# Half-empty filter blocks of two groups share one matmul, with tiles copied within SBUF; statistics by batch at the start of the convolutions; normalised rows gathered

## The reference

```python
def reference(x, ...):                       # x: (4, 512, 16, 32)
    x = x + _L0_conv_ref(_gn(x), gate_w, w1, w2, w3)
    x = x + _L1_conv_ref(_gn(x), w3, w7, w15, w_mix)
    x = x + _L2_conv_ref(_gn(x), ...)        # the same form, other weights
    x = x + _L3_conv_ref(_gn(x), ...)
    return x
```

## Time and profile before

| | |
|---|---|
| median of 3 runs | 1094.27 us (1093.65 to 1095.57) |
| the profiled execution | 1094.17 us, of which 1092.2 from the first to the last instruction |
| PE busy | 1040.1 us |
| DVE, ACT, POOL busy | 501.0, 318.4, 126.3 us |
| mean granted TensorE clock | 0.976 |
| experts, up to the last down product | about 705 us |
| convolutions | about 705 to 1092 us |

### The profile page before, as it was taken

One profiled execution on the slowest core, in us unless ns is written; L12 is line 12 of the kernel. 1 busy time (PEld: TensorE's weight loads), 2 busy tenths in 40 slices (PEclk: granted clock), 3 DMA queues, 4 the chain that ended last, 5 costly groups with the idle time before them and its releaser, 6 DMA issues.

```text
span 1092.2 us, 14489 instructions
## 1 busy us (share of the span) xinstructions
PE 1040.1 (95%) x5315; PEld 870.7 (80%) x5316; DVE 501.0 (46%) x700; ACT 318.4 (29%) x435; POOL 126.3 (12%) x169
## 2 busy tenths in 40 slices
PE   5589999999999999999999999779999999999998
PEld 3278888888888888888888888668888988898887
DVE  4794154155136155245164372266236942587011
ACT  2412144144144244144144352114201320122122
POOL 2031111111111211111111122100000000000000
PEclk9859999999999999999999999979999999999999
DMA  8309216943972985953976949755373466436474
GB/s 346 126 20 340 48 29 241 390 158 145 389 253 68 399 320 213 393 183 116 410 269 259 392 149 400 241 216 186 128 231 132 148 231 224 148 117 246 153 222 116
DMA packets 69792, 240.16 MB, mean 220 GB/s; under 512 B 6272, under 2 KB 36096, under 8 KB 55360
## 3 DMA queue, kind: packets, MB, share of 16 engines
q1 hardware_dynamic: 61536, 216.62, 52.1%
q0 software_dynamic: 8080, 23.07, 9.0%
q10 hardware_dynamic: 144, 0.02, 0.0%
HBM read 136.15 MB, written 107.74 MB: 223 GB/s over the span
## 4 chain that ended last, share of the span: by engine, by line
PE 83%; DVE 7%; issue 4%; DMA 3%; SPq 1%; ACT 1%; POOLq 0%; DVEq 0%; ACTq 0%; POOL 0%
PE gate_ps L977 15%; PE up_ps L977 15%; PE y_ps L964 10%; PE head_ps L1466 9%; PE head_ps L1470 9%; PE head_ps L1467 9%; PE y_ps L967 5%; PE hT_ps L989 2%; PE xT_ps L954 1%; PE xT_ps L886 1%; SPq L409 1%; DMA block_row<-in_x,fetch 1%; DVE scaled L1267 1%; DVE split L1277 1%; PE turn_ps L1416 1%
## 5 line engine op out<-in xcount | busy, mean ns | idle before, releaser
L1466 PE MATMUL head_ps<-split,ring 128*128 128x256 f32 (+1 forms) x657 | 225.4, 343 | 1.4 <-ACT split L1158 1.2
L1470 PE MATMUL head_ps<-split,ring 128*128 128x256 f32 (+1 forms) x657 | 220.6, 336 | 0.0
L1467 PE MATMUL head_ps<-split,ring 128*128 128x256 f32 (+1 forms) x657 | 220.1, 335 | 0.0
L977 PE MATMUL gate_ps<-front 128*128 128x512 f32 x560 | 177.3, 398 | 1.8 <-DVE xT_lo L810 1.7
L977 PE MATMUL up_ps<-front 128*128 128x512 f32 x560 | 173.8, 392 | 0.0
L1466 PEld LDWEIGHTS head_ps<-split,ring 128*128 128x128 f32 x657 | 124.4, 189 | 15.4 <-issue 2.1
L1470 PEld LDWEIGHTS head_ps<-split,ring 128*128 128x128 f32 x657 | 124.3, 189 | 14.6
L1467 PEld LDWEIGHTS head_ps<-split,ring 128*128 128x128 f32 x657 | 124.6, 190 | 13.6
L827 DVE TENSOR_TENSOR hidden<-silu,up_ps 128x1024 f32<-128x1024 f32 x35 | 42.8, 1222 | 177.9 <-ACT silu L586 177.9
L977 PEld LDWEIGHTS up_ps<-front 128*128 128x128 f32 x560 | 105.7, 189 | 22.9
L977 PEld LDWEIGHTS gate_ps<-front 128*128 128x128 f32 x560 | 102.9, 189 | 22.2 <-DVE xT_lo L810 2.1
(11 more groups left out here) (189 smaller groups left out, 1164.7 us busy)
## 6 DMA issues: line engine op xcount, KB each, us to landing
filters<-rows SPq DMA_DIRECT2D x56, 1568.0 KB
w_raw<-in_w13T SPq DMA_DIRECT2D x32, 1024.0 KB, 7.1
ring<-filters SPq DMA_DIRECT2D x15, 1920.0 KB, 7.9
w_raw<-in_w2T SPq DMA_DIRECT2D x16, 1024.0 KB, 5.2
ring<-filters SPq DMA_DIRECT2D x21, 768.0 KB, 4.7
ring<-filters SPq DMA_DIRECT2D x12, 1152.0 KB, 6.0
rows<-in_x SPq DMA_DIRECT2D x4, 1024.0 KB, 8.1
rowed<-acc SPq DMA_DIRECT2D x4, 1024.0 KB, 6.1
```

Of the source, the lines that this page charges most:

```text
L977: last = nc.tensor.matmul(o[:, n, :], a[:, k, :], b[:, k, t, n * 512:(n + 1) * 512], start=(k == 0 and a is xT_hi and b is w13_hi), stop=( ...
L1466: nc.tensor.matmul(place, kernel_hi, x_hi, start=(u == 0 and a == 0), stop=False)
L1467: nc.tensor.matmul(place, kernel_lo, x_hi, start=False, stop=False)
L1470: last = nc.tensor.matmul(place, kernel_hi, x_lo, start=False, stop=(u == len(units) - 1 and a == windows(s) - 1))
```

## The change

Three things.

**Shared half blocks.** Of a head's three units two have the same scale (`head_shared`). Their last windows, of which only partitions 64 to 127 count, become one product: partitions 64 to 127 hold the first one's filters and values, 0 to 63 the second one's. The filters are loaded into the two halves of a window of `ring` by two more DMAs of SP. The values are copied from partitions 64 to 127 of `split` into `shared` (4 slots) by POOL's DMAs, two for a task of 512 columns and four for one of 256, once the pieces are written and the slot is free. The three shared matmuls come last in a head and wait for them. A head thus has 5, 7, 8, 10 or 14 windows, and `ring` has 36 windows with new places.

**Statistics by batch at the beginning of the convolutions.** SP loads batch 0's rows when their own last block is added, then batch 1's. The filters of the second head wait for batch 1's rows. DVE does sums, centring and the subtraction batch by batch (`lane_sums`, `lane_centre`), then the factor for both (`lane_scale`). PE does a `lane_means` per batch and one `lane_deviations`, for batches 2 and 3 within the third task.

**Normalised rows gathered.** SP writes the normalised x to DRAM (`normal`) while routing runs, and POOL gathers blocks from there. `find_lanes`, `expand_lanes` and `normalise_rows` are gone. `find_weights` moves from the first block to its front, `take_targets` and `take_weights` ahead of the split of weight chunks 1 and 2, and that ahead of the low part of the first `xT`. POOL's copy of x to `acc` waits for x instead of the first expert's weights.

```diff
...
+def head_shared(h):
+    units = head_units(h)
+    return (0, 1) if units[0][0] == units[1][0] else (1, 2)
+def head_parts(h):
+    return [(s, j, windows(s) - (m in head_shared(h))) for m, (s, j) in enumerate(head_units(h))]
 def head_runs(h):
-    for s, j in head_units(h):
-        if runs and runs[-1][0] == s:
+    for s, j, n in head_parts(h):
+        if runs and runs[-1][0] == s and runs[-1][4] == n:
-            runs.append([s, j, 1, taken])
-        taken += windows(s)
+            runs.append([s, j, 1, taken, n])
+        taken += n
 def head_windows(h):
-    return sum(windows(s) for s, _ in head_units(h))
+    return sum(n for _, _, n in head_parts(h)) + 1
...
                if layer == l and same_batches(part, pair) and any(group == j for _, group in head_units(h)))
-RING = 48
-RING_PLACE = {11: 0, 12: 15, 6: 30, 13: 0, 14: 15, 15: 30, 10: 0, 7: 15, 8: 30, 9: 39, 0: 0, 1: 6, 2: 15, 3: 24, 4: 30, 5: 36}
+RING = 36
+RING_PLACE = {11: 0, 12: 14, 6: 28, 13: 0, 14: 14, 15: 0, 10: 14, 7: 28, 8: 0, 9: 16, 0: 8, 1: 24, 2: 0, 3: 14, 4: 19, 5: 28}
 for _i, (_l, _h) in enumerate(HEAD_SEQUENCE):
...
             if RING_PLACE[_head] < _at + head_windows(_h) and _at < RING_PLACE[_head] + head_windows(_head)]
-    RING_COUNT.append((_l + 1) * len(head_runs(_h)))
+    RING_COUNT.append((_l + 1) * (len(head_runs(_h)) + 2))
+SHARED = 4
+SHARED_AT = {h: i % SHARED for i, h in enumerate(HEAD_ORDER)}
+SHARED_PARTS = {None: (slice(0, 2),), 0: (slice(0, 1), slice(1, 2)), 1: (slice(0, 1), slice(1, 2))}
+SHARED_AFTER, SHARED_COUNT = [], []
+for _n, (_l, _h, _pair) in enumerate(TASKS):
+    SHARED_AFTER.append(max((_m + 1 for _m, (_, _head, _part) in enumerate(TASKS[:_n])
+                             if SHARED_AT[_head] == SHARED_AT[_h] and same_batches(_part, _pair)), default=None))
+    SHARED_COUNT.append(2 * len(SHARED_PARTS[_pair]) * sum(SHARED_AT[_head] == SHARED_AT[_h] and _part == _pair for _, _head, _part in TASKS[:_n + 1]))
...
             for k in range(KD):
+            for b in range(BATCH):
+                sp.wait_ge(normed, b + 1)
+                sp.dma_start(normal_rows[b], rows[:, b * QUARTERS:(b + 1) * QUARTERS, 0:D]).then_inc(normal_out, 16)
             for half in range(2):
+            sp.wait_ge(normal_out, 16 * BATCH)
...
-            pool.wait_ge(w13_in[KD - 1], 16)
+            pool.wait_ge(x_in[BATCH - 1], 16)
...
-                if isinstance(g, int):
-                    take_weights()
-            def new_expert(e, g0):
-                split_w13(e, g0, range(KD // 2))
-                normalise_rows(g0 + 1)
-                split_w13(e, g0, range(KD // 2, KD))
-            expand_lanes(0)
+            expand_weights()
-            expand_lanes(1)
-            take_lanes()
-            normalise_rows(0)
-            split_w13(0, 0, [1])
+            take_targets()
+            take_weights()
+            split_w13(0, 0, [1, 2])
-            split_w13(0, 0, range(2, KD))
-            expand_weights()
-            take_targets()
+            split_w13(0, 0, [3])
-            all_blocks(dve, new_expert, body, after_first)
+            all_blocks(dve, split_w13, body, after_first)
...
                 if RING_AFTER[i] is not None:
-                for s, j0, n, taken in head_runs(h):
-                    at, width = (RING_PLACE[h] + taken) * 2 * P, windows(s) * P
+                for s, j0, n, taken, count in head_runs(h):
+                    at, width = (RING_PLACE[h] + taken) * 2 * P, count * P
+                at = (RING_PLACE[h] + head_windows(h) - 1) * 2 * P
+                for half, m in zip((1, 0), head_shared(h)):
+                    s, j, count = head_parts(h)[m]
+                    begin = SCALE_AT[s] + count * P
+                    sp.dma_start(ring[half * P // 2:(half + 1) * P // 2, at:at + 2 * P].bitcast(f32).rearrange("p (a n) -> p a n", n=P),
+                                 filter_rows[P // 2:P, 2 * (l * GROUPS + j):2 * (l * GROUPS + j + 1), begin:begin + P]).then_inc(ring_in[h], 16)
-            wait_apart(sp, lasting.added, sp.value_load(table[0:1, E:E + 1], min_val=16, max_val=16 * (MAX_BLOCKS + 1)), lasting.sp_passed)
-            load_rows(0)
-            load_rows(1)
+            for b in range(PAIR):
+                wait_apart(sp, lasting.added, sp.value_load(table[0:1, E + b:E + b + 1], min_val=16, max_val=16 * (MAX_BLOCKS + 1)), lasting.sp_passed)
+                load_rows(b)
+            sp.wait_ge(rows_in[PAIR - 1], 16)
...
+        @block.gpsimd
+        def _(pool):
+            def share(n):
+                l, h, pair = TASKS[n]
+                slot, bs = SHARED_AT[h], batches(pair)
+                piece = l * len(PIECES) + max(PIECE_OF[head_units(h)[m][1], pair] for m in head_shared(h)) + 1
+                pool.wait_ge(high_ok, piece)
+                pool.wait_ge(low_ok, piece)
+                if SHARED_AFTER[n] is not None:
+                    pool.wait_ge(head_done, SHARED_AFTER[n])
+                for half, m in zip((1, 0), head_shared(h)):
+                    j = head_units(h)[m][1]
+                    for parts in SHARED_PARTS[pair]:
+                        pool.dma_start(shared[half * P // 2:(half + 1) * P // 2, slot, parts, bs.start:bs.stop, LEAD:LEAD + P].bitcast(f32),
+                                       split[P // 2:P, j, parts, bs.start:bs.stop, LEAD:LEAD + P].bitcast(f32)).then_inc(shared_in[slot, pair], 16)
+            for n in range(len(TASKS)):
+                share(n)
         def _(act):
...
                 for q in range(QUARTERS):
-            def lane_steps(pair):
-                at = LANE_STEPS * pair
-                dve.wait_ge(lane_step, at + PAIR * QUARTERS)
-                for b in range(PAIR):
-                    nc.vector.bn_aggr(lane[:, b, :], bn[:, b, :, :].rearrange("p q s -> p (q s)")).then_inc(lane_step, 1)
-                if pair == 0:
-                    nc.vector.memset(split[:, :, :, :, 0:LEAD].bitcast(f32), 0.0).then_inc(split_zeroed, 1)
-                group = lane_group[:, PAIR * pair:PAIR * (pair + 1), :]
-                dve.wait_ge(lane_stat, 2 * pair + 1)
-                nc.vector.tensor_copy(group.rearrange("p b s -> p (b s)"), stat_ps[:, 0, 0, 0:2 * PAIR]).then_inc(lane_step, 1)
-                dve.wait_ge(lane_step, at + PAIR * QUARTERS + PAIR + 1)
-                nc.vector.tensor_tensor(lane_dev[:, :], lane[:, :, 0], group[:, :, 0], ALU.subtract).then_inc(lane_step, 1)
-                dve.wait_ge(lane_step, at + PAIR * QUARTERS + PAIR + 2)
-                nc.vector.tensor_tensor(lane_dev2[:, :], lane_dev[:, :], lane_dev[:, :], ALU.mult).then_inc(lane_step, 1)
-                if pair == 0:
+                dve.wait_ge(lane_step, LANE_SUMMED[b] - 1)
+                nc.vector.bn_aggr(lane[:, b % PAIR, :], bn[:, b % PAIR, :, :].rearrange("p q s -> p (q s)")).then_inc(lane_step, 1)
+            def lane_centre(b):
+                n = b % PAIR
+                dve.wait_ge(lane_stat, LANE_MEANS[b])
+                nc.vector.tensor_copy(lane_group[:, b, :], stat_ps[:, 0, 0, 2 * n:2 * n + 2]).then_inc(lane_step, 1)
+                dve.wait_ge(lane_step, LANE_BEGUN[b] + 1)
+                nc.vector.tensor_tensor(lane_dev[:, n:n + 1], lane[:, n, 0:1], lane_group[:, b, 0:1], ALU.subtract).then_inc(lane_step, 1)
+                dve.wait_ge(lane_step, LANE_BEGUN[b] + 2)
+                nc.vector.tensor_tensor(lane_dev2[:, n:n + 1], lane_dev[:, n:n + 1], lane_dev[:, n:n + 1], ALU.mult).then_inc(lane_step, 1)
+                if b == 0:
-                for b in range(PAIR):
-                    at = (PAIR * pair + b) * P
-                    nc.vector.tensor_scalar(stream[:, :, at:at + P].rearrange("p j (q d) -> p j q d", d=HD),
-                                            rowed[:, PAIR * pair + b].rearrange("p q (j d) -> p j q d", d=HD),
-                                            group[:, b, 0:1], None, ALU.subtract).then_inc(first_ok, 1)
-                    if b == 0:
-                        dve.wait_ge(lane_stat, 2 * pair + 2)
-                        nc.vector.scalar_tensor_tensor(lane_var[:, :], stat_ps[:, 1, 0, 0:PAIR], EPS, group[:, :, 1], ALU.add, ALU.add).then_inc(lane_step, 1)
+                nc.vector.tensor_scalar(stream[:, :, b * P:(b + 1) * P].rearrange("p j (q d) -> p j q d", d=HD),
+                                        rowed[:, b].rearrange("p q (j d) -> p j q d", d=HD),
+                                        lane_group[:, b, 0:1], None, ALU.subtract).then_inc(first_ok, 1)
+            def lane_scale(pair):
+                dve.wait_ge(lane_stat, (PAIR + 1) * (pair + 1))
+                nc.vector.scalar_tensor_tensor(lane_var[:, :], stat_ps[:, 1, 0, 0:PAIR], EPS, lane_group[:, PAIR * pair:PAIR * (pair + 1), 1],
+                                               ALU.add, ALU.add).then_inc(lane_step, 1)
...
+            nc.vector.memset(split[:, :, :, :, 0:LEAD].bitcast(f32), 0.0).then_inc(split_zeroed, 1)
+            lane_centre(0)
-            lane_steps(0)
```

(39 more changed lines are left out.)

96 lines of the change are left out of this document (32 added, 64 removed).

## The result

| | before | after |
|---|---|---|
| median of four runs beside each other | 1094.92 us | 1126.64 us (1123.81 to 1137.7) |
| ratio, 95% interval | | 1.0306 [1.0254, 1.0359] |
| profiled execution, its span | 1094.17, 1092.2 | 1126.88, 1125.2 |

What follows compares the result with a forecast made beforehand. The convolutions were taken as bound by TensorE's number of matmuls and the columns they stream. The terms summed to -23.6 us from 1094.17, so 1070.6, stated as 1070; range 1057 to 1088.

Steps and rivals of the forecast that it cites:

- the ring's term: Filter loads through the ring cut from 48 to 36 windows, beside the copies: +1 us per layer, +3.0 in all.
- Rival B: Copies and ring loads meet, heads 12, 13 and 15 start late, 4 us per layer: 1079 us; chance 0.17.
- Full tasks: Copies for tasks of 512 columns: covered because pieces are written a task or more ahead; cost nothing.
- boundaries: Start of a new layer's half tasks, waiting for copies: +3.5 us at each of two boundaries, +7.0.
- first layer: First convolution layer's waits for copies: +2.4 us at head 12 and +1.9 at the second pair's first head.
- E+14.4: Head 11's forecast finish at a layer's start; E is the end of head 5, first pair, at 840.7 us.
- Matmuls removed: Three matmuls less per task in the convolutions, over three layers: -34.1 us where TensorE is the limit.
- Parts 2 and 3: Statistics by batch (-3.9 us at the convolutions' start, +1.5 for the second pair) and normalised rows gathered (-1.4).
- First head matmul: Start of the convolutions: about 717.3 us instead of 721.14, a gain of 3.9 us.
- the wait at the deviation matmul: Within head 6, TensorE stopped about 1.6 us for batch 2's whole subtraction; +1.5 us in the sum.
- The experts' start: First expert matmul at 76.4 us instead of 75.12, as VectorE splits weight chunks 1 and 2 first: +1.3.
- Rival A: POOL's queue becomes the bound at layer boundaries: +31 us each, about 1135; chance 0.08 for 1094 and above.

Runs made afterwards that it cites:

- spread: The changed kernel with every copy taken from and written to every other partition instead of the upper 64; 1081.0 us, ratio 0.9884.
- nocopy36: The changed kernel without copies, shared tiles filled once with zeros, ring still of 36 windows; 1068.3 us, ratio 0.9759 to the kernel before.
- ring40: The changed kernel with a ring of 40 windows and three shared slots instead of 36 and four; 1109.1 us, ratio 1.0135 to the kernel before.
- nocopy48: The changed kernel without copies, one zero-filled shared slot, and the ring of 48 windows in its old places; 1066.5 us, ratio 0.9736.
- best: The kernel pool with the last layer's outputs turned back later on TensorE; 1060.8 us, ratio 0.9693 to the kernel before.
- pool: The changed kernel with every copy into the shared tiles made by GpSimd itself instead of by DMA; 1074.5 us, ratio 0.9811.
- mixed: The changed kernel with the upper half of each shared tile copied by GpSimd itself, the lower half still by DMA; 1082.9 us, ratio 0.9890.
- stall: The kernel before, with head 15's filters in every layer loaded only when head 14 is done; 1124.0 us, ratio 1.0276.

## Why the prediction was wrong, step by step

**The step that failed is the ring's term,** "+1 us per layer, +3.0; bounds 0 and +4 per layer". It measured 34.4 us of waits, 11.5 a layer. Its reason had the bytes right, "8.4 MB per layer in runs of 512 bytes against 2.1 MB of windows saved", and went from them straight to "there is room on average". I never turned the bytes into DMA time, and the page of before had a price. Its q0 line, shown above, is 23.07 MB for 9.0% of 16 engines, 14.7 bytes per ns, where q1 gives 23.8. The copies' 25.2 MB at q0's price are 107 us of all engines in 371 us: 0.29 on top of 0.52. Measured were 0.84. That the two prices lie so close is partly luck: q0 of before holds gathers and accumulating writes of another kind, and the same copies cost 19.2 bytes per ns in spread. A share of 0.84 on average was 1.07 from 805 to 850 us, and a load with the 9.7 us of one head as its cover can't take 16.7.

**Rival B named the right place at a third of the size,** 4 us per layer against 11.5, and without the clock. It took one load of 10.3 us as the worst case, and called the ring the cause. The ring is innocent by itself (nocopy36), but it leaves less cover, so that delays become waits (ring40 takes back 17 us). What the copies cost beside a ring of 48 was not measured. "Full tasks: I cost these at nothing" is the same mistake seen from the other side. No full task's copy was late by itself, as I said; it made something else late.

**The second thing left out is the clock.** I priced waits by their idle time. PE is busy 351.6 us after and 332.3 in nocopy48 with the same 1933 instructions: 19.4 us of lower clock behind 46 us of waits. My list of signs did hold "a granted clock of 0.5 inside a layer", with no price beside it.

**The sum with what was measured:** ring +31.4 over its term, clock +19.4, boundaries +3.2 and first layer +0.8 (next point) make 54.8 of the 56.0 us. The matmuls' +3.3 and a start 1.2 earlier than forecast bring it to 56.9. That it closes within a microsecond is partly luck, since the boundaries' +3.2 is read off the first of the two alone.

**Boundaries.** Predicted +3.5 each. From the first matmul of head 3, second pair, to that of head 13 the kernel before takes 36.5 us (840.53 to 877.01), after 38.3 (851.91 to 890.24), and 3.2 less than before should be possible: +5.1. (At the second boundary it is 40.9 us, with a drop of the clock among them.) Head 11 ended at E+17.5, not E+14.4, since copies landed in 6.0 us beside the loads, not in 2 to 3. In nocopy48 the same stretch still takes 35.1 and in best 35.9: of the half tasks' 3.2 us, 1.8 and 2.6 are lost here even without DMA copies, and 1.7 of them are the wait of a total (`stat_ps`) for DVE's partial sums. The copies of the change cost the rest. The first layer's two waits were 2.4 and 2.7; I had 2.4 and 1.9.

**Matmuls removed.** Predicted -34.1, measured -30.8 in PE's busy time. A full head 13 takes 9.7 us from its first to its last matmul, as the prediction's sign asked. In best, which has no long wait, it is -31.9 (363.0 less 331.1); where the other 2.2 us went is open.

**Parts 2 and 3.** Predicted -3.8 in all, measured -3.4. First head matmul at 716.14 (717.3 predicted), the wait at the deviation matmul 1.5 (1.6). The 717.3 didn't follow from its own terms: they put the reciprocal 3.4 us earlier than before, which gives 717.8. The experts' start was missed: first expert matmul at 77.12, not 76.4, since the first rows came late, not DVE's splits. PE at that place after:

```profile
74.59 1.12 PE L928 MATMUL xT_ps<-ident,block_row 128*128 128x128 f32 x4 [4.57 <-DMA block_row<-normal,fetch]
77.12 1.22 PE L951 MATMUL gate_ps<-front 128*128 128x512 f32 x2 [1.41 <-DVE xT_lo L805]
```

**Rival A fell.** POOL's plain DMAs took 621 ns each (x204), beside a VectorE busy with two-input operations; 0.7 had been my figure. (Its +31 per boundary was also a slip: 59 less 26 is 33.) Of the two readings of the Trainium skill, "SBUF — State Buffer", Who interferes with whom, that the prediction set side by side, the trace agrees with the second: no starving beside `tensor_tensor`. But 1.09 us per DMA as the only way in which copies could hurt was too narrow.

**Left open.** Nocopy36 and nocopy48 stay 10 us and more above what I had worked out. Two waits and PE's busy time hold most of it in nocopy48, but why the turning back waits for ScalarE so much longer than before was followed only in pool. Copies issued from SP's or ACT's queue were not tried. Whether the average share or the partitions that copies and loads have in common makes the loads late was not separated.

## What to carry to other kernels

Price every new transfer in DMA-engine time, with the bytes per ns that the page's queue lines give for its kind, and add that share to the share of the stretch in which it runs. With the share near 1, loads with one step of cover become waits (11 in this kernel), and a wait of 7.4 us cost a third more through the clock. Here the copies within the on-chip store that touched half of the partitions were best left to an engine that had nothing to do.

## What the runs showed of the hardware that I had not expected

- A copy of 64 neighbouring partitions by DMA moved 13.9 bytes per ns of an engine, of 64 spread ones 19.2; the length of the runs made less of it (512 bytes 13.9, up to 4224 bytes 15.5).
- GpSimd copied 64 x 1024 elements out of partitions 64 to 127 in 1.15 us and 64 x 512 in 0.66, with half of the copies going to 0 to 63 (pool); with only those that stay in their partitions (mixed) it was 1.14 and 0.67.
- A GpSimd fill of 3.6 us stretched a VectorE subtraction of 1.28 us to 3.88 (nocopy36).
- Each of three waits of 7.4 us cost another 2.5 us at the lower clock (stall).
